# Attention scores as 64-row products of two head parities, with the row maxima turned on TensorE and sent by SP

## What is computed

```python
b, s, d = x.shape                                   # 8, 512, 256; 16 heads of 16
qkv = jnp.einsum('bsd,hde->bhse', x, Wqkv) + bqkv[None, :, None, :]
q, k, v = jnp.split(qkv, 3, axis=-1)
score = jnp.einsum('bhsd,bhtd->bhst', q, k)
causal = jnp.tril(jnp.ones((s, s), dtype=bool))
score = jnp.where(causal[None, None], score, -jnp.inf)
attn = jax.nn.softmax(score / jnp.sqrt(16.0), axis=-1)
y = jnp.einsum('bhst,bhtd->bhsd', attn, v)
```

## Time and profile before

| | us |
|---|---|
| median of 3 runs | 1206.84 (1206.24 to 1214.59) |
| profiled execution, its span | 1206.9 |
| TensorE, matrix products, busy | 1111.1 (92%), mean granted clock 0.98 |
| VectorE busy | 897.4 (74%) |
| ScalarE busy | 676.1 (56%) |
| GpSimd busy | 529.1 (44%) |

### The profile page before, as it was taken

The page is one execution under the profiler, slowest core; times in us unless marked ns, Lnnn a source line. Parts: engine busy times, 40 slices in busy tenths (PEclk is TensorE's granted clock), DMA queues, the critical chain, the costliest instruction groups (busy, mean ns, idle before and its releaser), DMA issues. The chain is left out here.

```text
span 1206.9 us, 26712 instructions
## 1 busy us (share of the span) xinstructions
PE 1111.1 (92%) x8873; PEld 745.7 (62%) x8905; DVE 897.4 (74%) x2217; ACT 676.1 (56%) x1463; POOL 529.1 (44%) x743
## 2 busy tenths in 40 slices
PE   4789999999999987998999999996999999999998
PEld 2345555555455546887999888983656646546555
DVE  5778887888888757975766657775876877877876
ACT  2256565555556564565656656664654664664653
POOL 5443434334243235844444444423646547447414
PEclk9689999999999999999999999998999999999999
DMA  5538544354533404665232453452241331331211
GB/s 146 112 67 237 102 80 98 80 111 96 93 81 80 99 19 155 215 179 165 79 127 83 119 163 124 126 149 85 89 141 36 106 126 48 105 102 64 96 45 62
DMA packets 105044, 129.36 MB, mean 107 GB/s; under 512 B 14976, under 2 KB 92736, under 8 KB 103936
## 3 DMA queue, kind: packets, MB, share of 16 engines
q1 hardware_dynamic: 93952, 109.27, 33.8%
q0 software_dynamic: 6912, 18.88, 5.6%
q10 hardware_dynamic: 4096, 0.14, 0.2%
HBM read 84.70 MB, written 43.38 MB: 106 GB/s over the span
## 5 line engine op out<-in xcount | busy, mean ns | idle before, releaser
L537 ACT ACTIVATE p<-bank 128x384 f32<-128x384 f32 (+1 forms) x384 | 191.9, 530 | 186.4 <-PE bank L937 118.8
L757 DVE TENSOR_REDUCE neg_max<-bank 128x1 f16<-128x384 f32 (+3 forms) x352 | 219.7, 640 | 64.7 <-PE bank L925 56.4
L452 POOL TENSOR_SCALAR_AFFINE_SELECT p<-p 128x256 f32<-128x256 f32 x256 | 104.1, 410 | 247.3 <-ACT p L537 246.7
L922 PE MATMUL bank<-k_stack,q_stack 96*128 96x384 f16 (+3 forms) x512 | 133.5, 313 | 20.1 <-DVE neg_max L757 13.1
L1377 POOL DMA_INDIRECT fetched<-xn_dram,token_now x80 | 81.2, 1015 | 42.8 <-POOL token_now L1373 30.6
L937 PE MATMUL bank<-q_stack,k_stack 97*128 97x512 f16 (+1 forms) x256 | 91.5, 362 | 6.0 <-ACT p L537 3.5
L2006 POOL TENSOR_TENSOR up_lo<-up_sq,up_hi 128x512 f16<-128x512 f32 x32 | 43.9, 1399 | 120.7 <-ACT up_hi L2063 120.7
L2017 POOL TENSOR_TENSOR he_lo<-he_sq,he_hi 128x512 f16<-128x512 f32 x64 | 79.9, 1268 | 36.7 <-ACT he_hi L2106 36.6
L1461 ACT ACTIVATE a<-xbank,b 128x256 f32<-128x256 f32 (+1 forms) x126 | 58.6, 468 | 51.2 <-PE xbank L149 47.8
L1549 DVE TENSOR_TENSOR h_lo<-h,h_hi 128x256 f16<-128x256 f32 x159 | 68.4, 433 | 24.4 <-ACT h_hi L1470 23.5
L955 PE MATMUL bank<-p,v_aug 128*32 128x512 f32 (+3 forms) x1024 | 83.5, 445 | 0.8 <-DVE o_rows L737 0.8
(11 more groups left out here) (342 smaller groups left out, 3375.2 us busy)
## 6 DMA issues: line engine op xcount, KB each, us to landing
w_bc<-wT_dram SPq DMA_DIRECT2D x8, 2048.0 KB, 8.0
y_routed_dram<-y SPq DMA_DIRECT2D x37, 256.0 KB
w<-in_w SPq DMA_DIRECT2D x10, 704.0 KB, 6.9
pack<-in_pack SPq DMA_DIRECT2D x12, 342.0 KB, 4.1
xr<-in_x SPq DMA_DIRECT2D x8, 512.0 KB, 7.3
xn_dram<-xn SPq DMA_DIRECT2D x8, 512.0 KB, 3.1
qk_hi_dram<-qk_hi SPq DMA_DIRECT2D x16, 256.0 KB, 2.4
qk_lo_dram<-qk_lo SPq DMA_DIRECT2D x16, 256.0 KB, 2.4
```

The lines of the kernel that those rows point to most:

```text
L452: pool.affine_select(out=diagonal, in_=diagonal, pattern=[[0, 2], [1, P]], compare_op=ALU.is_ge, fill=0.0, base=0, channel_multiplier=-1). ...
L537: act.activation(p32[:, s // GH % 2, s % GH, cols], s_bank[n][:, 0:cols.stop - cols.start], ACT.Exp).then_inc(p_exp.sem, 1)
L757: dve.tensor_reduce(neg_max[:, g % 2, 0:GH * TT].rearrange("p (h t) -> p h t", t=TT)[:, heads[0]:heads[-1] + 1, j], a_bank[c % 2][:, 0:len ...
L922: pe.matmul(to[:, at * w:(at + 1) * w], q_stack[0:STK, u, h0 + h, j * P:(j + 1) * P], k_stack[0:STK, u, h0 + h, 0:w], start=at == 0, stop= ...
```

## The change

- The stacks have 48 rows for a head and one for the maximum. Even heads lie in rows 0 to 48, odd heads in rows 64 to 112. All score products take 48 or 49 rows of one half. The clearings of the stacks are gone.
- `A_UNITS` has 12 units, each of one parity (two heads of j = 1, two of j = 0, or one head), in an order in which the unit of a slot has the other parity than `scores_k(s + 1, n)` of that slot.
- The causal mask is two products of 64 rows for each unit, from `mask_rows` and `mask_cols`, which `make_masks` builds on GpSimd at the start.
- The maxima of a group (128 x 16) are turned by a product with the identity in the next group's slot 1 (`turn_maxima`, on TensorE, into a score bank), copied by VectorE (`copy_turned`), and sent by SP in two transfers of eight rows of 256 bytes. VectorE's transposes and ScalarE's DMA issues are gone.
- DRAM holds the parts in stack order (`qk`, with three slots for each head). A half is stored with four transfers of high and two of low parts, 128 KB each with an outer dimension of 8 in DRAM, and fetched with four transfers of 48 rows.
- SP's list has `load_max` at fixed places between the stores and loads.

```diff
-STK, AUG = 96, 97
+STK, AUG = 48, 49
+HI_SLOTS, LO_SLOTS = ((0, 2), (1, 2)), ((1,), (0,))
+HALF = 64
+HEAD_PAIRS = NH // 2
...
-A_UNITS = (((0, 1, 2, 3), 0), ((0, 1), 1), ((2, 3), 1), ((0,), 2), ((1,), 2), ((2,), 2), ((3,), 2),
-           ((0,), 3), ((1,), 3), ((2,), 3), ((3,), 3))
+A_UNITS = ((0, (0, 1), 1), (0, (0, 1), 0), (0, (0,), 2), (1, (0, 1), 1), (1, (0, 1), 0), (1, (0,), 2),
+           (0, (0,), 3), (0, (1,), 3), (0, (1,), 2), (1, (0,), 3), (1, (1,), 3), (1, (1,), 2))
 AU = len(A_UNITS)
+TURN_BEFORE = 1
...
-AT_MAX = {0: (0, 1), 1: (2, 3)}
...
-        q_stack = sb("q_stack", [AUG, 2, NH, S], F16)
-        k_stack = sb("k_stack", [AUG, 2, NH, S], F16)
+        q_stack = sb("q_stack", [P, 2, HEAD_PAIRS, S], F16)
+        k_stack = sb("k_stack", [P, 2, HEAD_PAIRS, S], F16)
...
-        neg_max = sb("neg_max", [P, 2, 32], F16)
-        max_rows = sb("max_rows", [P, 2, 32], F16)
+        neg_max = sb("neg_max", [P, 2, GH * TT], F16)
+        max_rows = sb("max_rows", [GH * TT, 2, P], F16)
...
+        def units_before(g, i):
+
+            return (AU + 1) * g + i + (1 if i >= TURN_BEFORE else 0)
+
+        def turned_in(g):
+
+            return (units_before(g + 1, TURN_BEFORE) - 1) % 2
...
+            def store_slots(of, half, places):
+
+                for a, slots in enumerate(places):
+                    for r in slots:
+                        to = dram["qk"][a, half * NH // 2:(half + 1) * NH // 2, r]
+                        sp.dma_start(to, of[:, 2 * a + half, :]).then_inc(qk_stored.sem, 16)
+
             def store_hi(b, half):
-                hi_rows = dram["qk_hi"].rearrange("(a m p) s -> p m a s", a=2, p=P)[:, half]
-                hi_tile = qk_hi[:, :, :].rearrange("p (a m) s -> p m a s", a=2)[:, half]
                 sp.wait_ge(qk_hi_s.sem, qk_hi_s.at(b, 2 * half + 2))
-                sp.dma_start(hi_rows, hi_tile).then_inc(qk_stored.sem, 16)
-
-            def load_stacks(b, half):
-
-                u, heads = b % 2, slice(half * NH // 2, (half + 1) * NH // 2)
-                lo_rows = dram["qk_lo"].rearrange("(a m p) s -> p m a s", a=2, p=P)[:, half]
-                lo_tile = qk_lo[:, :, :].rearrange("p (a m) s -> p m a s", a=2)[:, half]
+                store_slots(qk_hi, half, HI_SLOTS)
+
+            def store_lo(b, half):
                 sp.wait_ge(q_lo_s.sem, q_lo_s.at(b, half + 1))
                 sp.wait_ge(k_lo_s.sem, k_lo_s.at(b, half + 1))
-                sp.dma_start(lo_rows, lo_tile).then_inc(qk_stored.sem, 16)
+                store_slots(qk_lo, half, LO_SLOTS)
+
+            def load_max(g):
+
+                b, pair0 = g // NG, GH // 2 * (g % NG)
+                sp.wait_ge(max_rows_s.sem, max_rows_s.at(g))
+                for par in range(2):
+                    row, of = HALF * par + STK, slice(GH // 2 * TT * par, GH // 2 * TT * (par + 1))
+                    to = q_stack[row:row + 1, b % 2, pair0:pair0 + GH // 2, :].rearrange("o h (t c) -> o (h t) c", t=TT)
+                    sp.dma_start(to, max_rows[of, g % 2, :]).then_inc(max_loaded[g % 2].sem, 16)
+
+            def load_stacks(b, half):
+
+                u, pairs = b % 2, HEAD_PAIRS // 2
                 sp.wait_ge(qk_stored.sem, qk_stored.at(2 * b + half))
                 if b >= 2:
-                    sp.wait_ge(s_psum.sem, s_psum.at((b - 2) * NH + heads.stop - 1))
+                    sp.wait_ge(s_psum.sem, s_psum.at((b - 2) * NH + (half + 1) * NH // 2 - 1))
+                if b == 0 and half == 0:
+                    fetch_heads(u, slice(0, GH // 2), first_heads_loaded)
+                    fetch_heads(u, slice(GH // 2, GH), stacks_loaded[half])
                 else:
-                    sp.wait_ge(stacks_cleared[b].sem, stacks_cleared[b].at(0))
-                if b == 0 and half == 0:
-                    fetch_heads(u, slice(0, GH), first_heads_loaded)
-                    fetch_heads(u, slice(GH, 2 * GH), stacks_loaded[half])
-                else:
-                    fetch_heads(u, heads, stacks_loaded[half])
-
-            def fetch_heads(u, heads, fetched):
-                hi, lo = (dram[k].rearrange("(a h d) s -> a d h s", a=2, d=HD)[:, :, heads, :] for k in ("qk_hi", "qk_lo"))
-                for r, (q, k) in enumerate(((hi, hi), (hi, lo), (lo, hi))):
-                    sp.dma_start(q_stack[HD * r:HD * r + HD, u, heads, :], q[0]).then_inc(fetched.sem, 16)
-                    sp.dma_start(k_stack[HD * r:HD * r + HD, u, heads, :], k[1]).then_inc(fetched.sem, 16)
+                    fetch_heads(u, slice(half * pairs, (half + 1) * pairs), stacks_loaded[half])
+
+            def fetch_heads(u, pairs, fetched):
+                heads = dram["qk"].rearrange("a (h w) r d s -> a w (r d) h s", w=2)
+                for par in range(2):
+                    for a, stack in enumerate((q_stack, k_stack)):
+                        sp.dma_start(stack[HALF * par:HALF * par + STK, u, pairs, :], heads[a, par, :, pairs, :]).then_inc(fetched.sem, 16)
...
+            load_max(0)
             for b in range(NB):
                 if b + 2 < NB:
                     load_x(b + 2)
+                load_max(NG * b + 1)
                 if b + 1 < NB:
                     store_xT(b + 1)
                     store_hi(b + 1, 0)
-                if b + 1 < NB:
+                    store_lo(b + 1, 0)
                     load_stacks(b + 1, 0)
+                load_max(NG * b + 2)
+                load_max(NG * b + 3)
                 if b + 1 == NB:
                     sp.wait_ge(xT_stored.sem, xT_stored.at(0))
                     load_shared()
                 if b >= 1:
                     store_x1(b - 1)
+                if b + 1 < NB:
+                    store_hi(b + 1, 1)
+                    store_lo(b + 1, 1)
                 if b + 2 < NB:
                     store_xn(b + 2)
                 if b + 1 < NB:
-                    store_hi(b + 1, 1)
                     load_stacks(b + 1, 1)
+                    load_max(NG * b + 4)
...
+            def make_masks():
+
+                flags, low, up = o_cols[:, 0, 0:3 * HALF], o_cols[:, 0, 3 * HALF:4 * HALF], o_cols[:, 0, 4 * HALF:5 * HALF]
+                eye, last = flags[:, HALF:P - 1], flags[:, 0:HALF]
+
...
+                pool.tensor_copy(mask_cols[:, :, :], low.unsqueeze(1).to_broadcast([P, 2, HALF])).then_inc(mask_made.sem, 1)
+
             inverse_std(0)
-            pool.wait_ge(w_lo.sem, 1)
-            clear(k_stack, 0)
+            make_masks()
...
-            def load_max(g, quarters):
-
-                b, h0 = g // NG, GH * (g % NG)
-                act.wait_ge(max_rows_s.sem, max_rows_s.at(g))
-                for q in quarters:
-                    to = q_stack[STK:AUG, b % 2, h0:h0 + GH, :].rearrange("o h (t q c) -> o q h t c", t=TT, q=4)[:, q]
-                    of = max_rows[32 * q:32 * q + GH * TT, g % 2, :]
-                    act.dma_start(to.rearrange("o h t c -> o (h t) c"), of).then_inc(max_loaded[g % 2].sem, 16)
...
             def maxima(g, i):
-                heads, j = A_UNITS[i]
-                c = AU * g + i
+                par, pairs, j = A_UNITS[i]
+                c = units_before(g, i)
                 dve.wait_ge(a_psum.sem, a_psum.at(g, i + 1))
                 w = (j + 1) * P
-                dve.tensor_reduce(neg_max[:, g % 2, 0:GH * TT].rearrange("p (h t) -> p h t", t=TT)[:, heads[0]:heads[-1] + 1, j],
-                                  a_bank[c % 2][:, 0:len(heads) * w].rearrange("p (x w) -> p x w", w=w), AX.X,
+                to = neg_max[:, g % 2, 0:GH * TT].rearrange("p (a h t) -> p a h t", a=2, t=TT)[:, par, pairs[0]:pairs[-1] + 1, j]
+                dve.tensor_reduce(to, a_bank[c % 2][:, 0:len(pairs) * w].rearrange("p (x w) -> p x w", w=w), AX.X,
                                   ALU.max, negate=True).then_inc(a_max.sem, 1)
-            def turn_maxima(g):
-
-                dve.wait_ge(a_max.sem, a_max.at(g))
+            def copy_turned(g):
+
+                dve.wait_ge(max_turned.sem, max_turned.at(g))
                 dve.wait_ge(max_loaded[g % 2].sem, max_loaded[g % 2].at(g // 2 - 1))
-                dve.transpose(max_rows[:, g % 2, :], neg_max[:, g % 2, :]).then_inc(max_rows_s.sem, 1)
+                dve.tensor_copy(max_rows[:, g % 2, :], a_bank[turned_in(g)][0:GH * TT, 0:P]).then_inc(max_rows_s.sem, 1)
...
-            clear(q_stack, 0)
...
             def scores_q(g, i):
-                b, h0, c = g // NG, GH * (g % NG), AU * g + i
+                b, pair0, c = g // NG, GH // 2 * (g % NG), units_before(g, i)
                 u, to = b % 2, a_bank[c % 2]
                 if i == 0 and g == 0:
                     pe.wait_ge(first_heads_loaded.sem, first_heads_loaded.at(0))
                 elif i == 0 and (g == 1 or g % 2 == 0):
                     half = g % NG // 2
                     pe.wait_ge(stacks_loaded[half].sem, stacks_loaded[half].at(b))
-                if c >= 2:
-                    pe.wait_ge(a_max.sem, c - 1)
-                heads, j = A_UNITS[i]
```

(42 more changed lines are left out.)

89 lines of the change are left out of this document (50 added, 39 removed).

## The result

| | before | after |
|---|---|---|
| median without profile, us | 1207.61 (4 runs) | 1305.82 (4 runs) |
| ratio | 1 | 1.0799 (95%: 1.0754 to 1.0844) |
| profiled execution, its span | 1206.9 | 1303.8 |

The change makes the kernel 8% slower. I had said 1209, with a range up to 1232.

A forecast was written before the change was run, and what follows sets the result against it. TensorE bounds attention now, VectorE close behind; after the change VectorE. A batch goes from 50.9 to 51.9 us: 1206.9 + 6 x 1.0 - 1 - 2.5 + 3 - 2 = 1210, stated as 1209, range 1176 to 1232.

The forecast's parts named there:

- the changes of shape: TensorE in attention: switching tile shape at 22 stretches a batch costs 2.0 to 4.2 us, taken as 3.
- the queue: SP's DMA queue: maxima land late behind stores and fetches, at T+12.5; TensorE stands 3.8 us in the first half.
- the batch without the queue: Attention batch without new waits: VectorE's 43.6 us plus 2.8 coupling loss, 46.4 us, 4.5 less than now.
- the turning product: TensorE, one new product a group that turns the maxima: 0.06 us each, 0.2 a batch.
- TensorE's saving: Score products in attention: key-side products run beside query-side ones on the other half of the array, -8.8 us a batch.
- The coupling of the two engines: TensorE and VectorE lock-stepping through two score banks: loss of 2.8 us a batch, 2 before.
- The half clock: TensorE slowed to 1.2 GHz after idling behind the stall for the maxima: +1.5 us a batch.
- The ends: Outside the steady batches: start -1 us, half clock at 66.9 -2.5, fill +3, last batch -2.
- the half clock at 66.9: Early slow stretch of TensorE, said to follow ScalarE's DMA issues and to go with them: -2.5 us.
- Fill: SP's queue: the 4 MB fill stands 16.8 us, now with a group's maxima behind it: +3 us, once.
- The stall decides: Rival: fetches stay at 6.4 us, maxima land at T+14.6, TensorE stands 5.9 us; 1235 us, chance 0.21.
- The slower cases: Rivals with a slower stall (1223 to 1240, chance 0.21) or halves running in turn (up to 1245, chance 0.08).

The follow-up runs named there:

- e1: The changed kernel with SP sending the maxima ahead of the stack fetches in both halves of a batch; 1270.5 us, ratio 1.050.
- e3: The changed kernel with maxima ahead of the fetches on SP and turned maxima in free columns of unit 2's score bank; 1253.5 us, ratio 1.0385.
- e5: e3 with the parities in the table of units exchanged, so that no products run side by side; ratio 1.077.
- e9: The kernel before with each unit's mask product on 64 rows instead of 128, adding changes of tile shape; ratio 1.0315.
- e7: The kernel before with VectorE's maxima taken over only the last 128 columns of each head; ratio 0.983.
- e8: e3 with VectorE's maxima taken over only the last 128 columns of each head; ratio 1.032.
- e11: e3 with the 4 MB fill issued in the last batch instead of the first; ratio 1.038.
- e6: e3 with each query-side score product of the last batch issued twice; ratio 1.041.

## Why the prediction was wrong, point by point

Of what slowed the kernel the prediction had two terms at their size: the changes of shape, and the queue with 5.5 us a batch (3.0 + 1.5 + 1.0), for which e1 gives 5.0. What failed is the batch without the queue, put at 46.4 us: with neither queue nor turning product in its way (e3) it lasts 54.4. And the turning product, put at 0.06 us a group, cost 17 to 18 us.

**TensorE's saving (failed).** The step was "the whole key side goes under the query side: -8.8". The mechanism is there, starts within 0.01 us. The size is not: 24 of 48 slots start both sides together. From e5 to e3 the fourth group loses 1.5 us of TensorE's work, 6 a batch if the others do as well, and 0.8 us of its length at full clock, 3.2 a batch. I compared columns of the two sides of a slot, but not when each is free to start. Waits of query-side products for the maxima stood in the earlier trace rows; each of them lets the key-side product go ahead alone.

**Changes of shape (right).** I took 3 us for 22 stretches. e9 gives 0.08 us for one change and 3.0 a batch, and e5 over the kernel before 0.75 us of work a group. The Trainium skill, "TensorEngine Tiling (Array Packing)", Key Properties, has the drain at a changed mode, and e9 agrees that a change has a price: nothing else was added there.

**The coupling of the two engines (failed).** VectorE's work came out as said: 217.2 us in five batches of e3, 43.4 each, for 43.6. But a batch without queue and bank is 54.4, not 46.4. A good 2 of the 8 us between are waits for stacks, which the edit of e1 makes later (10.8 us in five batches), and about 1 is the clock at 0.97. TensorE's work is 47.4 instead of 43. The rest is the loss by coupling, "I take 2.8": units wait for maxima 7.2 us a batch there (35.8 in five), against 3.3 before, and VectorE waits 3.6 (18.0 in five) for the turned maxima. e7 and e8 show the coupling's size, 0.5 to 0.8 us a group more than before. Why it grew is argued, not shown: short slots got shorter and long ones, with values in them, longer by the changes of shape, so VectorE would stand still during the long ones and set the pace in the short ones. No run had the new table of 12 units alone, so a part of it may be the table's order.

**The turning product (failed, unseen).** It had a price of 0.06 us a group. Taking it out of the exchange gave 17 to 18 us in all; 0.7 us a group at full clock, as the fourth group shows. The order of the waits was in the diff: unit 1 waits for `a_max.at(g, 1)`, the unit right before it. I priced the instruction, and not the bank it takes out of a pair.

**The queue on SP (right).** Stores at half rate: 163 GB/s. Fetches issued from T+6.7 (said 6.0), the last fetch landed at T+13.8 and the maxima in time for a product at T+14.2 (said T+12.5, bound T+14.6). TensorE waits 4.6 us a batch (said 4.8 for both halves, of which 4.0 lost). e1 gives 35 us for seven batches, 5.0 each, clock included.

**The half clock (mis-sized).** I took 1.5 us a batch behind one stall. The mean clock was 0.86, and with the queue away it stayed at 0.90. e1 shows what that costs: about 4 us a batch, with no stall by the queue left. The term had one stretch of half clock behind one stall; it came behind the many short waits as well.

**The ends (failed).** Start: said -1, came +2.4. Batch 0: said that the half clock at 66.9 goes; instead the batch has 0.69 of the clock and takes 7.1 us more. Fill: said +3; e11 shows it in the second batch and finds nothing in the whole time. Last batch: said -2, came +10.9, and in no edit of the changed kernel was it under 44 us. In the kernel after its clock is 0.72, and 7.9 of the 10.9 us are longer busy time of TensorE. The queue has little part in it: key-side products wait for the maxima's transfer once, 1.7 us, and the last group's maxima are ready 5.1 us before their product (6.4 in the kernel before). e6 speaks against lack of work between the waits. Why the clock is low there stays open.

**The rivals.** "The stall decides" had the right sign and mechanism, at 1235. None had two new waits at once, nor the bank. The slower cases held 0.28, and the range ended at 1232, since I let each of them stand alone. Two numbers there don't follow from the text: without the lower third of 1175 to 1195 the range starts at 1182, not 1176, and 0.34 and 0.02 are 0.36. Neither bears on the outcome.

## What to carry to other kernels

Running products side by side saves work of the engine, and time only where that engine doesn't then wait for another: here 2.2 us a group were promised, 1.5 of work saved, 0.75 spent on changes of shape, and what was left went into waits. Count the slots in which neither side waits, not the columns. A product that uses a buffer of an exchanging pair can cost a round trip of the exchange (0.7 us a group here), however short it is itself (0.06). And a small transfer that others need soon should stand ahead of a wait in its queue, not behind it: moving it ahead took 3% off here, and putting such transfers behind stores and fetches added 4% to the kernel before.

e7 is faster than both kernels (0.983). It leaves most of the maximum out; that is exact only as long as no score lies so far above its diagonal block's maximum that the exponential overflows. It shows what VectorE's reductions are worth, and is no replacement.
